# A decoder layer on one core: the first chunk ahead of the context's keys and values

## The reference, cut to what matters

```
x = x + gated_slot_attention(layernorm(x))      # 4 heads of 64, 64 slots, a recurrence over 512 steps
x = x + cross_attention(layernorm(x), ctx)      # 16 heads of 16, 64 context rows for each of the 8 batches
x = x + mixture_of_experts(layernorm(x))        # 8 experts, the best 2 for each token, capacity 1280
```

## Time and profile before

| | us |
|---|---|
| median of 3 runs | 1491.87 |
| lowest and highest of them | 1491.67, 1504.76 |
| time of the profiled execution | 1492.93 |
| its span, first to last instruction | 1491.2 |

### The profile page before, as it was taken

How to read it: one execution, slowest core, us unless ns; L and a number is a source line. 1 busy time by engine, 2 the same in 40 slices (tenths; PEclk the granted TensorE clock), 3 DMA queues, 4 the chain that set the end, 5 groups by cost and what they waited for, 6 DMA issues and landing times. The chain is left out here.

```text
span 1491.2 us, 32495 instructions
## 1 busy us (share of the span) xinstructions
PE 1371.4 (92%) x10841; PEld 1217.7 (82%) x10841; DVE 951.7 (64%) x3164; ACT 632.5 (42%) x1594; POOL 345.9 (23%) x524
## 2 busy tenths in 40 slices
PE   5799999899998999999866999999999999999995
PEld 3667777677777777777646999999999999999995
DVE  4468888788787878878754645555554655555442
ACT  1255455445445445445333434444343434444331
POOL 3112223132222323223210112121121212221122
PEclk9699999999999999999957999999999999999998
DMA  5341031011000001000003142231424232242111
GB/s 162 85 137 48 19 116 32 17 31 30 17 30 31 26 20 31 29 17 27 22 21 120 30 114 37 59 91 30 114 40 117 33 110 35 42 113 33 30 23 22
DMA packets 67292, 79.67 MB, mean 53 GB/s; under 512 B 11090, under 2 KB 60723, under 8 KB 67154
## 3 DMA queue, kind: packets, MB, share of 16 engines
q1 hardware_dynamic: 52562, 59.09, 13.0%
q0 software_dynamic: 14592, 18.91, 7.7%
HBM read 44.04 MB, written 33.96 MB: 52 GB/s over the span
## 5 line engine op out<-in xcount | busy, mean ns | idle before, releaser
L837 ACT ACTIVATE h_a<-banks 128x256 f32<-128x256 f32 x320 | 122.4, 383 | 352.2 <-PE banks L1319 350.6
L1253 DVE TENSOR_TENSOR h_f<-banks,h_a 128x256 f32<-128x256 f32 x320 | 135.5, 423 | 152.0 <-ACT h_a L837 146.9
L551 POOL TENSOR_TENSOR idle_g<-half 128x1 f32<-128x1 f32 x144 | 29.7, 206 | 699.7 <-DVE y_s L1272 391.3
L1319 PE MATMUL banks<-xe_t_hi,w_even_hi 128*128 128x256 f32 x640 | 179.8, 281 | 0.0
L1319 PE MATMUL banks<-xe_t_hi,w_odd_hi 128*128 128x256 f32 x640 | 178.6, 279 | 0.0
L1319 PE MATMUL banks<-xe_t_lo,w_even_hi 128*128 128x256 f32 x640 | 177.9, 278 | 0.0
L1319 PE MATMUL banks<-xe_t_hi,w_even_lo 128*128 128x256 f32 x640 | 177.8, 278 | 0.0
L1319 PE MATMUL banks<-xe_t_lo,w_odd_hi 128*128 128x256 f32 x640 | 177.0, 276 | 0.0
L1319 PE MATMUL banks<-xe_t_hi,w_odd_lo 128*128 128x256 f32 x640 | 176.9, 276 | 0.0
L826 ACT ACTIVATE h_t_hi<-h_f 128x256 fp32r<-128x256 f32 x320 | 131.8, 412 | 32.4 <-DVE h_f L1253 32.4
L1260 DVE TENSOR_TENSOR h_t_lo<-h_f,h_t_hi 128x256 fp32r<-128x256 f32 x320 | 133.5, 417 | 9.6 <-ACT h_t_hi L826 5.3
(11 more groups left out here) (240 smaller groups left out, 3518.2 us busy)
## 6 DMA issues: line engine op xcount, KB each, us to landing
raw<-in_w SPq DMA_DIRECT2D x24, 1024.0 KB, 5.8
expert_rows<-empty SPq DMA_DIRECT2D x4, 2580.0 KB, 11.3
xe<-expert_rows SPq DMA_DIRECT2D x40, 258.0 KB, 2.8
xin<-in_x SPq DMA_DIRECT2D x32, 128.0 KB, 2.4
out_dram<-x SPq DMA_DIRECT2D x32, 128.0 KB, 1.8
out_dram<-y_s,token POOLq DMA_INDIRECT x80, 3.8
mask_i<-in_mask SPq DMA_DIRECT2D x32, 32.0 KB, 1.8
expert_rows<-r_xn,send POOLq DMA_INDIRECT x64, 3.1
```

The source lines that it names most:

```text
L551: return pool.tensor_tensor(idle_g[:, i:i + 1], half[:, 0:1], half[:, 0:1], ALU.add)
L837: act.activation(h_a[:, f % 2, :], bank[2 + f % 4][:, 0:GS], ACT.Silu).then_inc(silu_ok, 1)
L1253: dve.tensor_tensor(h_f[:, f % 2, :], bank[2 + f % 4][:, GS:2 * GS], h_a[:, f % 2, :], ALU.mult)\
L1319: last = pe.matmul(dst, lhs, rhs, start=(i == 0), stop=(i == len(pairs) - 1))
```

## The change

- SyncE's first loads are chunk 0's x, `wv` and `wf` (counted by `vf_landed`), `wq` and `wk` (`qk_landed`), and only then the context and its two weights. The write and read back of the bias tables (`key_biases`) come after step 0, so ahead of the zero fills and of step 1.
- POOL makes the 9 constants that chunk 0 needs first (`chunk_consts`), does chunk 0's `f_power`, and then makes the other 27.
- PE's and DVE's prologues are gone. PE makes the keys and the first quarter of the values after `project_qk` of chunk 0, the second quarter after its `scores`, the other two after its `logits`, and the transpose for the query tables after its `read_out`. They are put in banks whose turn is free.
- DVE copies the context after chunk 0's `f_norm`, evacuates the value quarters ahead of `start_states`, after `causal_scores` and after `softmax_sum`, and makes `wo_s` and the bias tables after `causal_mix`.
- The keys' two evacuations go from DVE to ACT, after `ks_columns`.
- No computation is added or left out; from chunk 1 on the lists are the same as before.

The diff, cut to its core:

```diff
+        KEYS_AT = ("x_cols", "read")
+        VALUES_AT = ("values", "p_cols", "x_cols", "read")
...
+        vf_landed, qk_landed, chunk_consts = sem("vf_landed"), sem("qk_landed"), sem("chunk_consts")
...
-        CONSTS = 20 + XH
-        W_LOADS = 11 + B
+        CONSTS = 11 + XH
+        W_LOADS = 7 + B
+        CHUNK_CONSTS = 9
...
+            load_x(0, 0)
+            for j, w, landed in ((2, wv, vf_landed), (3, wf, vf_landed), (0, wq, qk_landed), (1, wk, qk_landed)):
+                sp.dma_start(w_in[:, :, j * D:(j + 1) * D], feat(w)).then_inc(landed, 16)
             sp.dma_start(ctx_s[:, :, :], feat(ctx_t)).then_inc(ctx_landed, 16)
             for j, w in ((1, xwk_t), (2, xwv_t)):
                 sp.dma_start(xw[:, j, :, :], feat(w)).then_inc(ctx_landed, 16)
-            load_x(0, 0)
-            for j, w in enumerate((wq, wk, wv, wf)):
-                sp.dma_start(w_in[:, :, j * D:(j + 1) * D], feat(w)).then_inc(w_landed, 16)
...
+            def key_biases():
+                sp.wait_ge(consts_step, CONSTS)
+                for j in range(PARTS):
...
+                    sp.dma_start(key_rows[rows, :, :], sl_wide[0:PARTS, j, :, :]).then_inc(sl_landed, 16)
+                sp.wait_ge(kb_step, 9)
+                sp.dma_start(key_dram.rearrange("i p k -> p i k"), kb_part[:, :, :]).then_inc(parts_stored, 16)
...
+                    sp.dma_start(query_dram[:, j * PARTS:(j + 1) * PARTS, :], qp_part[0:NCH, :, :]).then_inc(parts_stored, 16)
+                sp.wait_ge(parts_stored, 64)
+                load_key_rows(0)
+                load_places(0)
...
                 step(c // CPB, c % CPB)
+                if c == 0:
+                    key_biases()
                 if c < 4:
                     empty_rows(c)
-            sp.wait_ge(ctx_mm, 1 + B)
+            sp.wait_ge(ctx_mm, 1 + B // 2)
             sp.wait_ge(sl_landed, 16 * PARTS)
             load_expert(0)
...
+                    pool.wait_ge(used, n)
...
+            pool.memset(ident[:, :], 0.0).then_inc(chunk_consts, 1)
+            pool.memset(ones[:, :], 1.0).then_inc(chunk_consts, 1)
+            pool.memset(half[:, :], 0.5).then_inc(chunk_consts, 1)
...
+            pool.iota(expert_no[:, :], [[1, E]], base=0, channel_multiplier=0,
+                      allow_small_or_imprecise_dtypes=True).then_inc(chunk_consts, 1)
+            pool.wait_ge(chunk_consts, 3)
+            pool.affine_select(out=ident[:, :], in_=ident[:, :], compare_op=ALU.not_equal, fill=1.0,
+                               base=0, pattern=[[-1, P]], channel_multiplier=1).then_inc(chunk_consts, 1)
...
-            pool.memset(neg_half[:, :], -0.5).then_inc(consts_step, 1)
-            pool.memset(taken[:, :], 0.0).then_inc(consts_step, 1)
...
@@ -617,8 +629,12 @@
                         in_=r_xn[:, par, k, :], in_offset=None, bounds_check=SLOTS - 1, oob_is_err=False)\
                         .then_inc(sent[2 * par + k], 16)
...
         def _(act):
...
                 last.then_inc(et_ok, 1)
+            def context_keys(n, c, b):
+                if not later(n, 1):
+                    act.wait_ge(ctx_mm, 1)
+                    for k in range(KT):
+                        last = act.activation(k_all[:, k, :], tile[KEYS_AT[k]], ACT.Copy)
...
+            def double_context():
+                dve.wait_ge(ctx_landed, 48)
+                for k in range(KT):
+                    dve.tensor_copy(ctx2[:, k, :, :, :],
+                                    ctx_s[:, k, :].rearrange("p (b a k) -> p b a k", b=B, a=1).to_broadcast([P, B, 2, KL]))\
+                       .then_inc(ctx_doubled, 1)
+                dve.wait_ge(consts_step, CONSTS)
+            def context_values(part):
+                for b in range(part * B // 4, (part + 1) * B // 4):
+                    dve.wait_ge(ctx_mm, 2 + b // 2)
+                    dve.tensor_tensor(
+                        v_all[:, b, :, 0:2 * XD].rearrange("p j (i d) -> p j i d", i=2),
+                        tile[VALUES_AT[b // 2]][:, b % 2 * D:(b % 2 + 1) * D].rearrange("p (j i d) -> p j i d", j=PAIRS, i=2),
+                        pair_of[:, :].rearrange("p (a i b) -> p a i b", a=1, b=1).to_broadcast([P, PAIRS, 2, XD]),
+                        ALU.mult).then_inc(v_made, 1)
+                    dve.tensor_copy(v_all[:, b, :, 2 * XD:VW],
+                                    pair_of[:, :].rearrange("p (a i) -> p a i", a=1).to_broadcast([P, PAIRS, 2]))\
+                       .then_inc(v_made, 1)
...
+            def small_tables():
+                dve.wait_ge(w_landed, W_LOADS * 16)
+                for k in range(KT):
+                    dve.tensor_scalar(wo_s[:, k, :], wo_raw[:, k, :], gn[:, 0:1], None, ALU.mult).then_inc(small_made, 1)
+                dve.tensor_copy(qp[:, :], qp_i[:, :]).then_inc(qp_step, 1)
...
+                dve.wait_ge(qp_mm, 1)
+                dve.tensor_copy(qp_row[0:NCH, 0, :], tile["xy"][0:NCH, 0:P]).then_inc(qp_step, 1)
...
+            def f_norm_and_context(n, c, b):
+                f_norm(n, c, b)
+                if not later(n, 1):
+                    double_context()
+            def states_and_values(n, c, b):
+                if not later(n, 1):
+                    context_values(0)
+                start_states(n, c, b)
+            def sum_and_values(n, c, b):
+                softmax_sum(n, c, b)
...
+                    for part in (2, 3):
+                        context_values(part)
...
+            def scores_and_context(n, c, b):
+                causal_scores(n, c, b)
+                if not later(n, 1):
+                    context_values(1)
+            def mix_and_tables(n, c, b):
+                causal_mix(n, c, b)
+                if not later(n, 1):
+                    small_tables()
...
-            pe.wait_ge(qp_step, 1)
...
+            def context_keys():
+                pe.wait_ge(ctx_landed, 48)
+                for m in range(KT):
+                    last = product(tile[KEYS_AT[m]],
+                                   [(xw[:, 1, k, m * P:(m + 1) * P], ctx_s[:, k, :]) for k in range(KT)])
+                last.then_inc(ctx_mm, 1)
+                pe.wait_ge(ctx_doubled, KT)
+            def context_values(part):
+                for b in range(part * B // 4, (part + 1) * B // 4):
+                    last = product(tile[VALUES_AT[b // 2]][:, b % 2 * D:(b % 2 + 1) * D], [
+                        (ctx2[:, k, b, :, :].rearrange("p a k -> p (a k)"), xw[:, 2, k, :]) for k in range(KT)])
+                last.then_inc(ctx_mm, 1)
+            def query_positions():
+                pe.wait_ge(w_landed, W_LOADS * 16)
+                pe.wait_ge(qp_step, 1)
+                pe.wait_ge(v_made, 2 * B)
+                pe.transpose(tile["xy"][0:NCH, 0:P], qp[:, :], ident[:, :]).then_inc(qp_mm, 1)
+            pe.wait_ge(chunk_consts, CHUNK_CONSTS)
...
+                if not later(n, 1):
+                    pe.wait_ge(vf_landed, 32)
...
+                if not later(n, 1):
+                    pe.wait_ge(qk_landed, 32)
...
+                if not later(n, 1):
+                    pe.wait_ge(v_made, 2 * B // 4)
...
+                if not later(n, 1):
+                    pe.wait_ge(v_made, 2 * B // 2)
...
+                if not later(n, 1):
+                    pe.wait_ge(small_made, 2)
...
+                if not later(n, 1):
+                    pe.wait_ge(qp_step, 2)
...
+            def project_qk_and_context(n, c, b):
+                project_qk(n, c, b)
+                if not later(n, 1):
+                    context_keys()
+                    context_values(0)
+            def scores_and_values(n, c, b):
+                scores(n, c, b)
+                if not later(n, 1):
+                    context_values(1)
+            def logits_and_values(n, c, b):
+                logits(n, c, b)
+                if not later(n, 1):
+                    pe.wait_ge(k_made, 1)
+                    context_values(2)
+                    context_values(3)
+            def read_and_positions(n, c, b):
+                if not later(n, 1):
+                    pe.wait_ge(v_made, 2 * B)
+                read_out(n, c, b)
+                if not later(n, 1):
+                    query_positions()
```

## The result

| | before | after |
|---|---|---|
| median of 22 runs each | 1498.6 us | 1486.34 us |
| lowest and highest | 1489.46, 1505.86 | 1479.13, 1497.61 |
| ratio | | 0.9929, 95% interval 0.9909 to 0.9949 |
| span of the profiled execution | 1491.2 | 1482.9 |

The change makes the kernel 0.7% faster, 12.3 us by the medians and 10.6 by the ratio. The forecast was 12.0 less, at 1479.9, with a range up to 1486.0. The kernel before measured 1498.6 in 22 runs, among them the first three with their median of 1491.87, and so the changed kernel's median lies 0.34 above the range's end although the difference is close to the forecast one.

A forecast was written before the change was run, and what follows sets the result against it. It took the serial 20.9 us ahead of chunk 0 as the bound: 20.6 - 5.2 + 1.1 - 1.8 - 1.2 - 3.4 + 2.0 = 12.1, taken as 12.0, so 1491.87 - 12.0 = 1479.9 us. Range 1474.5 to 1486.

The forecast's parts named there:

- The terms for what the moved work costs inside chunk 0: Keys, value quarters and tables in chunk 0: 5.2 us ahead of gates, 1.8 ahead of logits, 1.2 behind, about 3.4 at its end.
- if the two leads differed: Sign: if chunk 1's `project_vf` (38.5) and chunk 2's (63.5 against 75.67) gain differently, chunk 1's clock is the reason.
- The landing: Front loads: the context's last part, now last of eight loads, lands at 9.9 us, 5.6 after issue.
- The cover that I named: Chunk 0: PE's wait for context and copy, until 12.1 us, hides behind `project_vf` and `project_qk`, lasting until 12.2.
- the last, from the sum to the time: Whole kernel: the 12.0 us gain taken off the earlier kernel's median, 1491.87, to give 1479.9.
- rival B: Chunk 0: inserted work costs more through late landing, DVE value quarters or slow clock; 3 to 7 us lost, 1483 to 1487; chance 0.12.
- The clock term: Chunk 0: PE runs at the higher granted clock, 2.4 GHz, which returns 2.0 us.
- a bound: Chunk 0's logits: 1.9 us at the higher clock, 3.3 at 1.2 GHz.
- A: Between chunks 0 and 1 the clock holds over PE's gap: 14.3 us earlier, 1477.6, or 16.3, 1475.6; chance 0.27.
- C: Chunk 0: the clock never rises before `causal_mix`; 15.7 us more, 1495.6, slower than before; chance 0.02.
- D: Start not on the path: row-buffer fills or experts' first weights end the chunk stage; nothing gained, 1491.9; chance 0.04.
- Nothing is taken back: Behind chunk 1: later loads and zero fills keep up, chunk 2's x with margin 9, so the 12.0 us lead stays.

The follow-up runs named there:

- e4: Changed kernel plus five idle 512-column products on PE behind chunk 0's `read_out`; 0.9927 of before.
- e9: Changed kernel with tables in DVE's idle places, three idle PE products behind chunk 0's `read_out` and three in chunk 1's gaps; 0.9880 of before.
- e8: Changed kernel with tables in DVE's idle places of chunk 0 and three idle PE products behind chunk 0's `read_out`; 0.9937 of before.
- e6: The changed kernel a second time, without any edit; 0.9952 of before.
- e5: Changed kernel with the tables moved from chunk 0's end into DVE's idle places of chunk 0, no fill; 0.9932 of before.
- e10: Changed kernel with tables and their transpose back ahead of chunk 0, and POOL's power behind all constants; not timed, traced span 1488.5 us.

## Why the prediction was wrong in the time, and where it was right

What failed is the level of the kernel before, taken from the median of three runs: 1491.87, where 22 runs give 1498.6. The schedule behind the difference held.

**The mechanism and the schedule held.** Point by point, forecast and first trace: `f_st` of chunk 0 3.2 and 2.81; `project_vf` 6.4 and 6.56; the first exponential 18.5 and 17.88; `lg` 24.9 and 24.26; `bt_s` 30.3 and 29.18; the tables 31.0 and 29.79, 4.3 long as forecast; chunk 1's statistic 35.3 and 34.08; its `project_vf` 38.5 and 37.42; chunk 2's 63.5 and 60.95. The terms for what the moved work costs inside chunk 0 were each right to within 0.8. Chunk 2's further 1.5 are the clock of chunk 1, as the forecast had said it would be if the two leads differed: low from 33.5 to 40.4 here, from 38.0 to 55.1 in the trace of before.

**The landing was wrong and cost nothing.** The context's last part was put at 9.9 and came at 11.52, 7.3 after its issue in place of 5.6. PE's keys followed at 11.65, when `project_qk` was through. The cover that I named was just enough: DVE's `g_s` started at 13.32, 1.8 behind the end of the ACT step that it needs (11.51), and PE did not ask for it until 16.6.

**The step that failed is the last, from the sum to the time.** "From the median, which lies 1.06 lower, 1491.87 - 12.0 = 1479.9" takes three runs for the level of the kernel before. In the 22 of the comparison, six lie at or below 1491.87; the median is 1498.6, 6.7 above the level that the forecast started from, and in three more comparisons it was 1494.78 (25 runs), 1496.82 (23) and 1499.69 (11). The forecast's own 12.0 off 1498.6 gives 1486.6, against 1486.34 measured. That also lies within rival B's 1483 to 1487, but by the level and not by B's costs. The median of three drawn from the 22 lies between 1491.7 and 1503.1 eight times in ten. The range was built of the bounds of the mechanism alone, 1474.5 to 1486.0, and nothing in it stood for that, although a run at 1504.76 was on the table. The difference, not the level, was what the trace could give.

**The clock term was one draw.** The sum credited 2.0 for the higher clock and took 50.44 as the start of chunk 1. The other trace of before has 49.19 there and 92.30, not 96.64, at chunk 3; in one of three traces of the changed kernel the clock fell in chunk 0 after all, from 22.6 to 26.0. It hit the second quarter of the values (3.53 in place of 1.99) and not the logits, for which the forecast had kept a bound; with the later first rise it cost 3.0 at chunk 1, the size of rival B's lower end. Over the traces at hand the lead at chunk 3 is 94.5 less 83.8, 10.7, and the timed lead some 9. So 12.0 was the high side of a right size, and the 12.3 by the medians of the first comparison agree with it partly by luck.

**The rivals.** A (the clock holds over the gap) did not occur by itself in three traces; filled by hand it gave 1.5 within chunk 1's `project_vf` (e4), and with chunk 1's gaps filled too chunk 3 came at 79.29 and 78.65, 2.5 to 8.9 ahead of the changed kernel's three traces. C and D did not occur: three traces had the high level for most of chunk 0, and the lead stands at the end. "Nothing is taken back" held on the chain: in the first traces the lead is 14.9 at chunk 3 and 13.4 at the first group (787.03 against 800.43). The experts' pace (below) takes the next 5.3. The chunks behind chunk 3 scatter as well: from there to the first group the changed kernel's three traces took 705.3, 700.7 and 707.8, before's 703.8 and 704.3.

**Left open.** Why the experts' pace changes level, and whether something in the start favours one level. No run here changed only that. The timed gain of e9 over e8, 9.8 us, is over twice the lead that their traces show, and that is open too.

## What to carry to other kernels

Lay the first pass of a loop out as a schedule, engine by engine, with the trace's own durations: it was right to 1.2 us over 35 in the first trace. Where two chains stand side by side in front, expect little from moving one: here the tables alone gained 1.5 to 2.8 us at chunk 1 and the context alone nothing, both together 9 to 13. Give the level of a time its own width, from the scatter of its runs, and let the schedule give only the difference. In a stretch where the matmul engine waits on others, look at the granted clock before shortening a chain: here 2.8 us less of chain gave no gain that the runs can tell (0.9932), and eight idle products in the gaps gave 0.9881.

## What was not expected of the hardware

**The experts' groups have two paces.** In the same code, at a granted clock of 1.00, one group takes 16.79 and another 17.37. The stretches of a group each, in the trace of the changed kernel (columns as above):

```profile
899.92:916.71 16.79, 16.79 (x150) 16.79 (x149) 10.19 (x24) 7.91 (x20) 3.73 (x5) 1.00 0.20 32
1205.96:1223.33 17.37, 17.37 (x151) 17.37 (x150) 7.95 (x22) 6.12 (x17) 3.47 (x4) 1.00 0.68 213
...
1240.10:1257.50 17.40, 17.40 (x151) 17.40 (x150) 10.19 (x24) 7.91 (x19) 3.47 (x4) 1.00 0.19 32
```

And one of the trace of before:

```profile
1218.30:1235.08 16.78, 16.78 (x151) 16.78 (x150) 7.91 (x22) 6.12 (x17) 3.93 (x4) 1.00 0.72 220
```

PE is full in all; its records follow one another at 0.113 us in the groups of 16.8 and at 0.118 in those of 17.4. The DMA traffic does not make the difference: a group of 17.4 has 32 GB/s and one of 16.8 has 220. Every second group takes 17.4 once that mode has begun, and in all traces the level changed either at the first groups or between group 19 and group 22. With no group, half of the stage or all of it in that mode the groups take 652, 658 or 664.6. That is 13 us between executions whose experts' part is the same, more than the change brings; within one program the two traces of before lie 6.4 apart.

**The granted clock's first rise and its falls are tied to the program only in part.** It rose at 9.6 to 12.4 in kernels with the same start, fell in chunk 0 in some executions (low from 22.6 to 26.0 in e6 and e9) and not in others, and fell at 33.8 in a gap of 1.9 (e5). The same wait of PE in chunk 1 goes with a fall at 54.0 in the changed kernel (2.07 of idle time before 53.00) and with none in e10:

```profile
62.00:64.00 2.00, 0.38 (x3) 0.38 (x4) 1.38 (x5) 0.54 (x2) 0.00 (x0) 1.00 0.00 0
```

```profile
63.62 0.44 PE L1364 MATMUL banks<-ident,b_p 128*128 128x128 f32 x2 [2.08 <-DVE b_p L1055]
```

The Trainium skill (TensorE: Matmul & The Clock Gate, "What's actually happening") has the low clock as the default that activity releases; the fills agree. The page also has the moment of the first rise vary from run to run; the changed kernel's three traces show it, at 9.6, 12.4 and 9.9.
